# Attention stage of a four-layer graph network: which engine issues the loads of the edge weight rows

## The chip, the cores and the metric

The kernel runs on one core of a Trainium2 chip. The metric is device time in microseconds (us). The engines are TensorE (PE), VectorE (DVE), ScalarE (ACT), GpSimd (POOL) and SyncE (SP). Each runs its own instruction stream, and they meet only at semaphores. SP and ACT can issue ordinary DMAs, POOL issues the gathers whose rows are chosen by an index.

## The reference, cut to what matters

Four message-passing layers follow each other on a graph of 6250 nodes and 206250 edges, with a layer norm after each. The change lies in the fourth:

```python
w_ij = _mlp(edge_feats, rad_w0, rad_b0, rad_w1, rad_b1)
w_ij = w_ij + _mlp(chi_scalar, sph_w0, sph_b0, sph_w1, sph_b1)
q = (node_feats @ wq).reshape(-1, H, HD)[receivers]
k = (node_feats @ wk).reshape(-1, H, HD)[senders]
alpha = (q * w_ij * k).sum(axis=-1) / jnp.sqrt(jnp.float32(HD))
alpha = alpha * cutoffs[:, None]
v = (node_feats @ wv).reshape(-1, H, HD)[senders]
out = jax.ops.segment_sum(alpha[..., None] * v, receivers, num_segments=n_nodes)
```

`w_ij` does not depend on the nodes, so the kernel computes it ahead: one unit of the edge network gives the 512 rows of one group and stores them in the DRAM tensor `w_dram`.

## The kernel before

Edges are sorted by receiver and cut into 404 groups of 512 edges (4 tiles of 128). The attention stage (`attention_edges`) walks over them in 101 iterations `i` of 4 groups, `s` = 0 to 3, each with its own buffers in `kv_rows`, `w_rows`, `msgs` and `hot`. The other layers come before it; most units of the edge network are computed in them, and the last 110 in the attention stage: two in each of the first 14 iterations (`twos`), one in each of the next 82, none in the last 5. These three kinds are called the two-unit, one-unit and no-unit iterations.

What each engine does for a group `s`, in its program order:

- SP loads the weight rows of the group (256 KB, `load_w`, line 1854) once the message of the group four back is done, then the sender indices of the group four ahead (line 1849) when the gathers of this one have landed, then the receiver lanes (line 1846) when VectorE has turned the lanes before them into marks. After the four groups it stores the finished unit of the edge network (line 891) and loads the features of the next (line 882).
- POOL waits for the message of the group four back and issues four gathers of 128 key and value rows each (line 1917).
- TensorE picks the queries of the group (line 1927, waits for `hot_t` and for the message two back), adds up the messages of the group before (line 753), and does a quarter of the edge network. In a one-unit iteration that is, for `s` = 0 and 1, two of the four chunks of its first layer (line 909), and for `s` = 2 and 3 half of its second layer (line 918). In a two-unit iteration it is a whole first layer for `s` = 0 and 2 and a whole second layer for `s` = 1 and 3.
- ScalarE makes the marks of the group for the sums (`lane_hot`, lines 726 and 729, into `att_hot`), then runs Silu over the chunks that TensorE has just made (line 929, `late_hid`).
- VectorE multiplies weight rows and keys (line 2040, it waits there for the weight rows and the gathers), multiplies the queries in (line 2044, it waits for `q_done` of TensorE), reduces over heads (line 2045) and forms the message (line 2047, it counts `msg_done`). Around this it makes the windows of queries (lines 1992 and 1994), the marks `hot_t` of a group ahead (line 1984), adds finished sums into the nodes (lines 741 and 742) and finishes the edge network's rows (lines 935 and 938).

ScalarE's order in a one-unit iteration is therefore: marks 0, Silu of chunks 0 and 1, marks 1, Silu of chunks 2 and 3, marks 2, marks 3. The rows of a unit may be read only when its store has landed; SP waits for that itself, at iterations 73 and 90 and before the no-unit iterations (`mlp.stored`, `mlp.finished`).

Of the kernel before, what the change touches and what calls it, by code (L numbers as in the profile page):

```python
# [17 lines left out]
D = 128  # L18
# [3 lines left out]
T = 4  # L22
GE = T * P
S = 4
NI = -(-E // (S * GE))
# [694 lines left out]
def lane_hot(nc, act, c, s, g):  # L720

    hot = c.hot[:, s]

    act.wait_ge(c.sums_done, g + 1)
    for t in range(T):
        ins = nc.scalar.activation(hot[:, t, :], c.iota[:, 0:P], ACT.Square, scale=-1.0, bias=c.spans.lane_near[:, bass.ds(g * T + t, 1)])
    ins.then_inc(c.square_done, 1)
    act.wait_ge(c.square_done, g + 1)
    nc.scalar.activation(hot, hot, ACT.Relu, scale=-1.0, bias=1.0).then_inc(c.hot_done, 1)
# [1064 lines left out]
def attention_edges(nc, a, iota, own_lane, spans, lo_dram, w_dram, q_parts, kv_dram, acc, mlp):  # L1794


    with ExitStack() as st:
        sem = nc.alloc_semaphore

        def sb(name, shape, dt=f32):  # L1800
            return st.enter_context(nc.sbuf_tensor(f"att_{name}", shape, dt))
# [3 lines left out]
        twos, ones = 14, 96  # L1805
        units = 2 * twos + ones - twos
        assert mlp.start + units == NG

        def unit_of(i, per):
            return 2 * i if per == 2 else i + twos  # L1810
        kv_rows = sb("kv_rows", [P, S, T, 2 * D])
        w_rows = sb("w_rows", [P, S, T, D])
# [12 lines left out]
        msg_done = sem("att_msg_done")  # L1825
# [12 lines left out]
        w_in = [sem(f"att_w_in{s}") for s in range(S)]  # L1838
        lanes_in = [sem(f"att_lanes_in{s}") for s in range(S)]

        with nc.Block() as block:

            @block.sync
            def _(sp):
                def load_lanes(s, g):
                    sp.dma_start(lanes[:, s], lo_dram[bass.ds(g * GE, GE)].partition_broadcast(P)).then_inc(lanes_in[s], 16)

                def load_indices(s, g):
                    sp.dma_start(stage[:, s], a["src_tiles"][:, bass.ds(g * T, T)]).then_inc(staged[s], 16)

                def load_w(s, g):

                    sp.wait_ge(msg_done, g + 1)
                    sp.dma_start(w_rows[:, s].rearrange("p t f -> p (t f)"),
                                 w_dram[:, bass.ds(g * T * D, T * D)]).then_inc(w_in[s], 16)

                for s in range(S):
                    load_indices(s, s)
                for s in range(S):
                    load_lanes(s, s)  # L1860
                def body(i, per, first):
                    for s in range(S):
                        load_w(s, S * i + s)

                        sp.wait_ge(gathered[s], 16 * T * (i + 1))
                        load_indices(s, S * (i + 1) + s)

                        sp.wait_ge(hot_t_done, S * i + s + 1)
                        load_lanes(s, S * (i + 1) + s)
                    if per:  # L1870
                        mlp.sync_body(sp, unit_of(i, per), per, first)

                body(0, 2, True)
                with sp.Fori(1, twos) as i:
                    body(i, 2, False)
                with sp.Fori(twos, 73) as i:
                    body(i, 1, False)

                mlp.stored(sp, 80)
                with sp.Fori(73, 90) as i:  # L1880
                    body(i, 1, False)

                mlp.stored(sp, 100)
                with sp.Fori(90, ones) as i:
                    body(i, 1, False)
                mlp.store(sp, units - 1)
                mlp.finished(sp, units - 1)
                with sp.Fori(ones, NI - 1) as i:
                    body(i, 0, False)
                for s in range(S):  # L1890
                    load_w(s, S * (NI - 1) + s)

            @block.scalar
            def _(act):
                def body(i, per):
                    for s in range(S):
                        lane_hot(nc, act, c, s, S * i + s)
                        if per:
                            mlp.scalar_step(nc, act, unit_of(i, per), s, per)

                with act.Fori(0, twos) as i:
                    body(i, 2)
                with act.Fori(twos, ones) as i:
                    body(i, 1)
                with act.Fori(ones, NI) as i:
                    body(i, 0)

# [243 lines left out]
```

## Time and profile before

| | |
|---|---|
| runs | 11267.62 us, median of 3 (11256.81 to 11269.58) |
| profiled execution | 11251.21 us, its span 11249.4 us |
| granted TensorE clock | 0.828 of full speed over the span |
| busy, share of the span | PE 73%, DVE 57%, ACT 44%, POOL 28% |
| attention stage | about 8240 to 11191 us of the span |

The span is from the program's first instruction to its last. Busy time is that of an engine's own instructions; waits, branches and the issuing of DMAs by SP and ACT are not counted. A row of the timeline gives start, duration, engine, line, operation and in brackets the idle time of the engine before it with what ended it. In this kernel one and the same semaphore can serve two stages, so the name of a releaser can be that of an earlier user.

### The profile page before, as it was taken

To read this page: it belongs to the slowest core of one execution; us is meant where nothing else is said; L and a number is where in the kernel's file an instruction comes from. 1 tells how busy PE (TensorE), PEld (TensorE's weight loads), DVE (VectorE), ACT (ScalarE), POOL (GpSimd) and SP (SyncE) were. 2 spreads that over 40 slices of the span, in tenths; PEclk is the share of its full clock that TensorE was granted. 3 is DMA by queue.
4 is the path that set the end of the run, shared out by engine and by line. 5 is a ranking of instruction groups with operands and counts; after the bars stand their busy time and mean duration, and the time that the engine had idled before them with its cause. 6 is when DMAs were issued, how large, how long until landed. Compare 5 with 4: busy or idle time off the path is not lost. (4 is left out here: it accounts for less than half of the span.)

```text
span 11249.4 us, 197335 instructions
## 1 busy us (share of the span) xinstructions
PE 8246.0 (73%) x51344; PEld 6196.6 (55%) x51345; DVE 6369.1 (57%) x11872; ACT 4935.1 (44%) x9054; POOL 3183.7 (28%) x3246
## 2 busy tenths in 40 slices
PE   3888888878869999994777777777657565656654
PEld 2555555567757777773555554554435454444443
DVE  5777777789943333335555555555655555555555
ACT  2444444468745555552333333333434333333332
POOL 0000000000000000000555555555235555555554
PEclk9889888899989999996777777777778777777776
DMA  2222222256623333331111111111045445454544
GB/s 80 104 104 104 103 105 102 104 174 227 213 92 122 119 122 123 118 105 31 43 43 43 43 43 43 43 43 43 19 133 149 143 142 143 143 145 141 143 144 115
DMA packets 634626, 1180.46 MB, mean 105 GB/s; under 512 B 215640, under 2 KB 295818, under 8 KB 615011
## 3 DMA queue, kind: packets, MB, share of 16 engines
q1 hardware_dynamic: 505288, 861.87, 24.0%
q0 software_dynamic: 129280, 317.93, 10.0%
q8 instruction: 24, 0.39, 0.0%
q14 instruction: 34, 0.28, 0.0%
HBM read 902.78 MB, written 276.57 MB: 105 GB/s over the span
## 5 line engine op out<-in xcount | busy, mean ns | idle before, releaser
L1708 POOL DMA_INDIRECT conv_rows<-y_dram,conv_stage x1616 | 1550.8, 960 | 4064.3 <-issue 3399.5
L1917 POOL DMA_INDIRECT att_kv_rows<-kv_dram,att_stage x1616 | 1625.4, 1006 | 1563.0 <-DVE att_msgs L2047 845.6
L753 PE MATMUL conv_part<-conv_msgs,conv_hot 128*128 128x256 f32 x3232 | 1060.2, 486 | 159.3 <-DVE conv_msgs L1771 115.0
L929 ACT ACTIVATE late_hid<-att_mlp,late_b 128x512 f32<-128x512 f32 x440 | 282.2, 684 | 1789.3 <-remote 821.0
L1688 ACT ACTIVATE conv_hid<-conv_hid_ps 100x512 f32<-100x512 f32 x406 | 240.2, 592 | 1731.1 <-remote 866.4
L1076 DVE SCALAR_TENSOR_TENSOR mean_rest<-mean_counts,mean_high 128x896 f16<-128x896 f32 x343 | 374.7, 1093 | 1077.7 <-ACT mean_high L1037 1077.7
L1721 PEld LDWEIGHTS conv_w_ps<-conv_w,conv_hid 100*128 100x128 f32 x3240 | 509.9, 240 | 831.8 <-ACT conv_hid L1688 549.3
L918 PE MATMUL att_mlp<-late_w,late_hid 128*128 128x128 f32 x3520 | 583.0, 334 | 504.2 <-ACT late_hid L929 457.8
L753 PEld LDWEIGHTS conv_part<-conv_msgs,conv_hot 128*128 128x128 f32 x3232 | 765.3, 249 | 321.7 <-DVE conv_msgs L1771 118.1
L1721 PE MATMUL conv_w_ps<-conv_w,conv_hid 100*128 100x128 f32 x3240 | 602.4, 343 | 461.9 <-ACT conv_hid L1688 448.2
L293 PE MATMUL count_ps<-count_cols,count_rows 128*128 128x392 bf16 x3920 | 802.8, 354 | 159.2 <-DVE count_cols L259 158.3
L918 PEld LDWEIGHTS att_mlp<-late_w,late_hid 128*128 128x128 f32 x3520 | 547.8, 245 | 530.2 <-ACT late_hid L929 478.8
L2044 DVE TENSOR_TENSOR att_qk<-att_q_ps,att_qk 128x512 f32<-128x512 f32 x404 | 279.5, 692 | 950.9 <-DMA conv_scalars<-in_scalars 805.5
L753 PE MATMUL att_part<-att_msgs,att_hot 128*128 128x128 f32 x3232 | 577.9, 334 | 324.1 <-DVE att_msgs L2047 251.9
L918 PE MATMUL count_mlp<-mlp_w,mlp_hid 128*128 128x128 f32 x4704 | 691.0, 315 | 142.5 <-DVE mlp_w L938 140.5
L918 PEld LDWEIGHTS count_mlp<-mlp_w,mlp_hid 128*128 128x128 f32 x4704 | 678.9, 230 | 189.4 <-issue 166.3
L1123 PE MATMUL mean_sum_ps<-wh,mean_turned 128*128 128x129 f32 x4802 | 696.5, 285 | 51.9 <-ACT mean_turned L1045 51.3
L293 PEld LDWEIGHTS count_ps<-count_cols,count_rows 128*128 128x128 bf16 x3920 | 380.1, 103 | 642.2 <-issue 449.1
L318 ACT ACTIVATE count_counts<-count_ps 128x784 f32<-128x784 f32 x392 | 322.7, 823 | 864.6 <-PE count_ps L293 857.8
L753 PEld LDWEIGHTS att_part<-att_msgs,att_hot 128*128 128x128 f32 x3232 | 501.5, 237 | 364.0 <-issue 198.4
L259 DVE TENSOR_SCALAR count_cols<-cols,col_key 128x784 bf16<-128x784 f16 x1960 | 687.0, 419 | 0.0
L577 PE MATMUL soft_ps<-wh,soft_weights 128*128 (+1 forms) x4802 | 579.9, 280 | 142.7 <-DVE soft_weights L521 142.7
(278 smaller groups left out, 16499.4 us busy)
## 6 DMA issues: line engine op xcount, KB each, us to landing
c_dram<-count_counts SPq DMA_DIRECT2D x392, 392.0 KB, 2.4
mean_counts<-c_dram SPq DMA_DIRECT2D x343, 448.0 KB, 3.6
att_w_rows<-w_dram SPq DMA_DIRECT2D x404, 256.0 KB
soft_counts<-c_dram SPq DMA_DIRECT2D x98, 1024.0 KB, 4.8
w_dram<-mlp_w SPq DMA_DIRECT2D x294, 256.0 KB, 2.5
mlp_feats<-in_feats SPq DMA_DIRECT2D x295, 192.0 KB, 2.7
soft_counts<-c_dram SPq DMA_DIRECT2D x49, 1088.0 KB, 5.0
att_lanes<-lo_dram SPq DMA_DIRECT2D x404, 128.0 KB
```

Source lines behind the costliest of these rows:

```text
L259: ins = nc.vector.tensor_scalar(c.cols[:, b, t], at.cols[:], at.col_key[:, bass.ds(first + t, 1)], None, ALU.is_equal)
L293: ins = nc.tensor.matmul(c.ps[:, b, h, 0:CW // 2], rows, cols[:, h * (CW // 2):(h + 1) * (CW // 2)], start=first, stop=last)
L318: nc.scalar.activation(c.counts[:, v % 4].rearrange("p (h c) -> p h c", h=2), ps, ACT.Copy).then_inc(c.copied, 1)
L577: ins = nc.tensor.matmul(place(m), weights[:, b, m * P:(m + 1) * P], win(wh, w), start=False, stop=False, skip_group_check=True)
L753: ins = nc.tensor.matmul(part, c.hot[:, s, t, :], rows[:, t, :], start=half == 0 and t == 0, stop=half == 1 and t == T - 1)
L918: ins = nc.tensor.matmul(self.w_ps[:, t * D:(t + 1) * D], self.hid[:, n, t * P:(t + 1) * P], self.w1[:, n, :], start=n == 0, stop=n == 2 * ...
L929: nc.scalar.activation(self.hid[:, n], self.hid_ps[:, n % 2], ACT.Silu, bias=self.b0[:, n:n + 1]).then_inc(self.hid_done, 1)
L1076: nc.vector.scalar_tensor_tensor(rest[:, m], counts[:, m], 0.25, high[:, m], ALU.mult, ALU.subtract).then_inc(rest_done, 1)
L1123: ins = nc.tensor.matmul(sum_ps[:, 0:D + 1], turned[:, h, at:at + P], x_ext[:, k, :], start=k == 0, stop=k == NW - 1)
L1708: pool.indirect_dma_start(rows[:, s, t, :], None, y_dram, bass.IndirectOffsetOnAxis(ap=stage[:, s, t:t + 1], axis=0)).then_inc(gathered[s] ...
L1721: ins = nc.tensor.matmul(w_ps[:, n, t, :], hid[:, n, t * P:(t + 1) * P], w2[:], start=True, stop=True)
L1917: pool.indirect_dma_start(kv_rows[:, s, t, :], None, kv_dram, bass.IndirectOffsetOnAxis(ap=stage[:, s, t:t + 1], axis=0)).then_inc(gathere ...
```

## The change

`load_w` goes from SP's stream to ScalarE's. There it stands behind the marks of the same group and before the Silu of the chunks. The waits for the stores of the edge network's units go with it, and the loop of the one-unit iterations is split on ScalarE where it was split on SP. SP waits for the last loads at the end.

```diff
                 def body(i, per, first):
                     for s in range(S):
-                        load_w(s, S * i + s)
-
                         sp.wait_ge(gathered[s], 16 * T * (i + 1))
                         load_indices(s, S * (i + 1) + s)
...
-                with sp.Fori(twos, 73) as i:
-                    body(i, 1, False)
-
-                mlp.stored(sp, 80)
-                with sp.Fori(73, 90) as i:
-                    body(i, 1, False)
-
-                mlp.stored(sp, 100)
-                with sp.Fori(90, ones) as i:
+                with sp.Fori(twos, ones) as i:
                     body(i, 1, False)
...
                 for s in range(S):
-                    load_w(s, S * (NI - 1) + s)
+                    sp.wait_ge(w_in[s], 16 * NI)
 
             @block.scalar
             def _(act):
+                def load_w(s, g):
+
+                    act.wait_ge(msg_done, g + 1)
+                    act.dma_start(w_rows[:, s].rearrange("p t f -> p (t f)"),
+                                  w_dram[:, bass.ds(g * T * D, T * D)]).then_inc(w_in[s], 16)
+
                 def body(i, per):
                     for s in range(S):
                         lane_hot(nc, act, c, s, S * i + s)
+                        load_w(s, S * i + s)
                         if per:
                             mlp.scalar_step(nc, act, unit_of(i, per), s, per)
...
+                with act.Fori(twos, 73) as i:
                     body(i, 1)
+
+                mlp.stored(act, 80)
+                with act.Fori(73, 90) as i:
+                    body(i, 1)
+
+                mlp.stored(act, 100)
+                with act.Fori(90, ones) as i:
+                    body(i, 1)
+                mlp.stored(act, units - 1)
```

## Rows read from the trace of the kernel before

**Rows 1.** Windows: us; busy PE, PEld, DVE, ACT, POOL; clock; DMA; GB/s.

```profile
8240.00:8689.00 449.00, 320.11 (x2211) 239.26 (x2212) 244.00 (x445) 205.87 (x416) 230.93 (x235) 0.81 0.51 148
8689.00:11061.00 2372.00, 1431.06 (x9876) 1168.52 (x9874) 1333.12 (x2462) 804.08 (x1982) 1326.46 (x1312) 0.74 0.50 143
```

**Rows 2.** Waits of VectorE, one-unit iterations; us in total, times, longest.

```profile
DVE att_qk L2044 <- DMA conv_scalars<-in_scalars: 710.8, 154, 7.1
```

**Rows 3.** Tile att_w_rows, whole trace: idle before its reader until the load landed.

```profile
  DMA att_w_rows<-w_dram: 8.0, 13
```

**Rows 4.** Timeline of one one-unit iteration, VectorE.

```profile
10020.64 0.69 DVE L2047 TENSOR_TENSOR att_msgs<-att_kv_rows,att_alpha 128x512 f32<-128x512 f32 x1
...
10024.18 0.69 DVE L2047 TENSOR_TENSOR att_msgs<-att_kv_rows,att_alpha 128x512 f32<-128x512 f32 x1
...
10029.35 0.69 DVE L2040 TENSOR_TENSOR att_qk<-att_w_rows,att_kv_rows 128x512 f32<-128x512 f32 x1
...
10031.52 0.75 DVE L2047 TENSOR_TENSOR att_msgs<-att_kv_rows,att_alpha 128x512 f32<-128x512 f32 x1
...
10039.66 0.69 DVE L2044 TENSOR_TENSOR att_qk<-att_q_ps,att_qk 128x512 f32<-128x512 f32 x1 [6.45 <-DMA conv_scalars<-in_scalars]
...
10044.94 0.69 DVE L2040 TENSOR_TENSOR att_qk<-att_w_rows,att_kv_rows 128x512 f32<-128x512 f32 x1
...
10047.66 0.69 DVE L2044 TENSOR_TENSOR att_qk<-att_q_ps,att_qk 128x512 f32<-128x512 f32 x1 [2.04 <-DMA conv_scalars<-in_scalars]
...
10049.11 0.69 DVE L2047 TENSOR_TENSOR att_msgs<-att_kv_rows,att_alpha 128x512 f32<-128x512 f32 x1
```

**Rows 5.** Timeline of the same iteration, TensorE and ScalarE.

```profile
10023.28 2.02 PE L909 MATMUL att_mlp<-late_feats,late_w 64*128 64x512 f32 x4
...
10025.33 1.26 ACT L929 ACTIVATE late_hid<-att_mlp,late_b 128x512 f32<-128x512 f32 x2 [8.21 <-issue]
...
10026.94 1.13 PE L909 MATMUL att_mlp<-late_feats,late_w 64*128 64x512 f32 x4
...
10027.78 0.63 ACT L729 ACTIVATE att_hot<-att_hot 128x512 f32<-128x512 f32 x1
...
10029.68 0.83 PE L1927 MATMUL att_q_ps<-att_q_both,att_hot_t 128*128 128x128 bf16 x12 [1.60 <-DVE att_hot_t L1984]
...
10037.97 0.69 ACT L929 ACTIVATE late_hid<-att_mlp,late_b 128x512 f32<-128x512 f32 x1 [9.56 <-issue]
10039.43 0.69 ACT L929 ACTIVATE late_hid<-att_mlp,late_b 128x512 f32<-128x512 f32 x1 [0.78 <-remote]
...
10041.32 0.63 ACT L729 ACTIVATE att_hot<-att_hot 128x512 f32<-128x512 f32 x1
...
10043.75 1.49 PE L1927 MATMUL att_q_ps<-att_q_both,att_hot_t 128*128 128x128 bf16 x12
```

**Rows 6.** Timeline of the same iteration, POOL: first and last gather of two runs.

```profile
10022.11 0.94 POOL L1917 DMA_INDIRECT att_kv_rows<-kv_dram,att_stage  x1 [2.90 <-DVE att_msgs L2047]
...
10036.83 0.95 POOL L1917 DMA_INDIRECT att_kv_rows<-kv_dram,att_stage  x1 [0.30 <-issue]
10042.58 0.94 POOL L1917 DMA_INDIRECT att_kv_rows<-kv_dram,att_stage  x1 [4.81 <-DVE att_msgs L2047]
...
10046.74 0.94 POOL L1917 DMA_INDIRECT att_kv_rows<-kv_dram,att_stage  x1 [0.30 <-issue]
```

**Rows 7.** Timeline, two-unit iterations: a weight load, and the reader that waits for it.

```profile
8374.43 0.34 SPq L1854 DMA_DIRECT2D att_w_rows<-w_dram  x1
...
8377.53 0.69 DVE L2040 TENSOR_TENSOR att_qk<-att_w_rows,att_kv_rows 128x512 f32<-128x512 f32 x1 [0.26 <-DMA att_w_rows<-w_dram]
```

**Rows 8.** Timeline of that two-unit iteration, later: query waits and the last marks.

```profile
8383.67 0.69 DVE L2044 TENSOR_TENSOR att_qk<-att_q_ps,att_qk 128x512 f32<-128x512 f32 x1 [5.45 <-DMA conv_scalars<-in_scalars]
...
8406.68 0.69 DVE L2044 TENSOR_TENSOR att_qk<-att_q_ps,att_qk 128x512 f32<-128x512 f32 x1 [5.24 <-PE att_q_ps L1927]
8407.65 0.63 ACT L729 ACTIVATE att_hot<-att_hot 128x512 f32<-128x512 f32 x1
```

More of the change, by code:

```diff
@@ L1849, in load_indices @@
                     sp.dma_start(stage[:, s], a["src_tiles"][:, bass.ds(g * T, T)]).then_inc(staged[s], 16)
[L1851 to L1855, printed above, removed]
                 for s in range(S):
@@ L1902, in _ @@
                     body(i, 2)
-                with act.Fori(twos, ones) as i:
+                with act.Fori(twos, 73) as i:
                     body(i, 1)
+                mlp.stored(act, 80)
[5 more added lines that the diff above has]
+                mlp.stored(act, units - 1)
                 with act.Fori(ones, NI) as i:
```

## The prediction

> **What bounds the kernel now.** Only the attention stage is touched. Its windows come first: two-unit iterations take 449 us for 14 (32.1 us each), one-unit ones 2372 us for 82, or 28.9 us each [rows 1]. No engine is full there: POOL and VectorE are each busy 56% of the time, ScalarE 34%, the DMA engines 50% [rows 1]. So waits bound it. VectorE's waits come next: it stands 711 us before L2044, the multiply by the picked queries [rows 2]. The releaser's name is that of an earlier user of the semaphore; by the code it is `q_done` of TensorE. Weight rows cost nothing yet: in the whole stage their reader lost 8.0 us to them [rows 3].
>
> The timeline of one iteration shows what the 711 us are. I count from the end of the last message of the iteration before, 10020.64 + 0.69 = 10021.33, as t = 0 [rows 4]. The period is 28.5 us here: the fourth message ends at 10049.80. Two stalls stand in it: 6.45 us before L2044 of s = 2 and 2.04 us before that of s = 3 [rows 4].
>
> The first is odd. TensorE's picks for s = 2 end at t = 9.2 and its chunks 2 and 3 at 6.7, yet VectorE starts L2044 at 18.3, and ScalarE the two Silu at 16.6 and 18.1 [rows 4, 5]. Both come just after POOL's row of twelve gathers ends, at t = 16.45 [rows 6]. The second stall has the same look: the picks end at t = 23.9, POOL's next row of four ends at 26.35, and L2044 starts at 26.3 [rows 4 to 6]. In the first 3 us of a row nothing is held: chunks 0 and 1 end at t = 3.97 and the Silu starts at 4.00 [rows 5]. I read it so: what TensorE signals from some 3 us after the start of a row of gathers arrives only when the row pauses, 0.2 to 1.9 us later. The cause is not shown; the pattern is what I use.
>
> **The change, part by part.** *SP* loses four issues of about 0.34 us per iteration [rows 7] and the order they imposed. SP holds up nobody I can name, as indices and lanes are loaded a group or more ahead: nothing, and it would cost nothing back. The waits for the stores, now on ScalarE, stand before iterations 73 and 90 and before the no-unit ones, for units long stored: three waits, under 1 us each. In the five no-unit iterations the marks run ahead of VectorE: nothing.
>
> *ScalarE* gets four issues, about 0.35 us each with their register work. It is busy a third of the time; I count the 0.35 us only where a chain runs through it. Queued behind each issue are the next Silu and marks, for which TensorE waits.
>
> *The load's lead* is the real change. A load needs 3.1 us from issue to its reader's start (8374.43 to 8377.53) [rows 7]. Below, 2.8 us is left without the 0.34 us of its issue; above, one gather's cadence more, (10036.83 - 10022.11) / 11 = 1.3 us [rows 6], for a load that shares the DMA engines with a row of gathers: 4.4 us. I take 3.1, the measured one. ScalarE issues it when the last step of the marks has started. Walk through the one-unit iteration:
>
> - s = 1: the last step of the marks starts at 10027.78, t = 6.45 [rows 5]. Issue 6.8, landed 9.9. The reader wanted it at t = 8.0 [rows 4]: a new wait of 1.9 us. The message of s = 1, which ended at 10.94, ends at 12.8.
> - That opens the row of gathers. Eight of twelve are done at t = 11.2 (twelve end at 16.45, the last four take 5.1 us like the row of four [rows 6], with a 0.2 us start). POOL restarts 0.78 us after a message [rows 4, 6], at 13.6: a pause of 2.4 us. The held signals arrive in it, up to 1.65 us after its start, as before (39.43 against 37.78) [rows 5, 6]. Silu of chunks 2 and 3 starts by 12.9.
> - s = 2: from the second Silu to the last step of the marks it took 41.32 - 39.43 = 1.9 us [rows 5]. So issue at 12.9 + 1.9 + 0.35 = 15.1, landed 18.2. L2040 then and L2044 0.7 us later, at 18.9, against 18.3 before. The stall of 6.45 us is thus not won: the weight rows take its place, 0.6 us later. The message ends at 21.05 (before 20.5).
> - s = 3: L2040 follows the message by 3.15 us as before (10044.94 against 10041.8) [rows 4], at 24.2; its rows landed at about 21. TensorE has had chunks 2 and 3 activated since 13.6, so the picks for s = 3, formerly ending at 23.9, end by 20, in the pause between the row that ends at 18.8 and the message of s = 2. The 2.04 us stall is gone: L2044 at 24.9, message done at 27.05.
>
> The period falls from 28.47 to 27.05 us, by 1.4 us; times 82, -115 us.
>
> *Two-unit iterations.* The load for s = 3 is issued after marks whose last step starts at 8407.65 [rows 8], so it lands at 8411.1, and L2044, which started at 8406.68, starts at 8411.9: +5.2 us. But the next iteration's L2044 waits 5.45 us for the picks [rows 8], which TensorE then has done meanwhile. That gives about 5.4 back. The wait of 1.9 us at s = 1 I carry over whole. Net +1.7 us, times 14, +24 us; ends 0 and 14 x 7.1 = +99 us if nothing is given back.
>
> Sum: -115 + 24 = -91 us on the profiled execution's 11251.2 us (span 11249.4), 11160. The median of the runs lies 16.4 us above that execution, so **11177 us**.
>
> **A rule that speaks against it.** The weight rows would now arrive last at s = 1 and 2 of each one-unit iteration, where before the whole stage lost 8.0 us to them [rows 3]. The Trainium skill, "DMA: Bandwidth & Descriptors", Rules for kernel authors, asks to issue a DMA early and wait late, so that its fixed cost lies beside other work. By that rule the change only loses. The same table says that spreading DMAs over engines brings no bandwidth and saves issue time alone; with the DMA engines half idle I count no bandwidth either.
>
> **Rivals.**
>
> 1. *The row of gathers doesn't pause* (slower). If the load for s = 1 lands by about t = 8.5, the pause is shorter than the 1.65 us that the second Silu needed; or signals stay held through it. Then the second Silu starts at 18.1 as before, the load for s = 2 is issued at 20.35 and lands at 23.45, L2044 starts at 24.15 instead of 18.3, +5.8 us; the 2.04 us of s = 3 go: +3.8 us x 82 + 24 = +336, **11604 us**. For it: 16 gathers are POOL's constant work, and the load may be issued up to a microsecond sooner than here. Against: 1.9 us of new wait stand in the rows.
> 2. *The hold moves forward* (slower). With the period shorter, the row of s = 2 ends at 26.9 and the next starts at 27.8, a pause of 0.9 us where it was 2.9 us [rows 6]. If chunks 0 and 1 are then held too, their Silu starts at 12.9, the load of s = 1 lands at 18.2, that of s = 2 at 21.7, the last message ends at 30.6: +2.1 us x 82 + 24 = +196, **11464 us**.
> 3. *Fewer loads beside the gathers, no hold of chunks 2 and 3* (faster). The load that SP issued at the start of the row is gone. If the hold sets in after t = 6.7, the load of s = 2 lands by 13, and the stall moves to s = 3, whose picks are held until the merged row ends at about 23.9: last message at 26.1, -2.4 us x 82 + 24 = -173, **11095 us**.
> 4. *No change in kind*: the weight rows hide in the stalls and the waits trade places, 0 x 82 + 0 to 24, **11268 to 11290 us**.
>
> **Chances.** The forecast 0.35, rival 3 0.13, rival 4 0.12, rival 2 0.18, rival 1 0.22. About 0.2% (22 us) is what a measurement of this kernel can tell from no change. The faster cases are 0.48; of rival 4 and the edges of the others 0.11 is the same; slower 0.41. The forecast's own range is 11120 to 11240, the period shorter by 2.1 to 0.6 us: the landing of 2.8 to 4.4 us moves the s = 2 step by -0.3 to +1.3. The range of 8 in 10 runs from 11070 to 11580: it holds rivals 2 and 3 and half of rival 1, which lies by what share of the iterations fall into it.
>
> **What would show it.** Right: in one-unit iterations VectorE waits before L2040, not L2044, about 1.9 us at s = 1 and longer at s = 2; POOL's rows are of eight, four and four gathers; Silu of chunks 2 and 3 near t = 12; no stall at s = 3; a period near 27. In two-unit iterations a wait of some 10 us before the last L2040 and none before the first L2044. Wrong: rows of twelve still there with L2040 of s = 2 near t = 23; Silu of chunks 0 and 1 later than t = 5; or no waits for `att_w_rows` at all.

## The result: slower by 1.7%

The kernel before takes 11,265.8 us (median of 4 runs, 11,256.8 to 11,269.6), the changed one 11,455.0 us (4 runs, 11,440.7 to 11,473.8). The ratio is 1.017, 95% interval 1.0152 to 1.0188; a second measurement gave 1.0188, 1.0171 to 1.0205. The forecast was 11,177 us with a range of 11,070 to 11,580: wrong side, inside the range.

The profiled execution of the changed kernel has a span of 11,451.1 us at a granted clock of 0.820, against 11,249.4 us at 0.828. First the windows of its two-unit and one-unit iterations (us; busy time and count by engine; clock; DMA share; GB/s), which answer to [rows 1]:

```profile
8265.00:8795.00 530.00, 344.06 (x2244) 256.41 (x2244) 245.13 (x445) 210.62 (x422) 234.45 (x236) 0.77 0.43 126
8795.00:11261.00 2466.00, 1549.40 (x9839) 1266.37 (x9840) 1345.46 (x2462) 814.33 (x1963) 1321.00 (x1312) 0.74 0.48 137
```

VectorE, ScalarE and POOL do the same work in more time. Iteration by iteration, from the end of one fourth message to the next, a two-unit iteration takes 36.8 us instead of 31.2 (mean of the last 13), a one-unit one 30.07 instead of 28.92 (mean of 82): 13 x 5.6 = 73 and 82 x 1.15 = 94 us. The first two-unit iteration adds about 7 us. The remaining 27 us lie ahead of the attention stage, whose first message ends at 8248.4 us in one profile and at 8274.9 in the other. Over the twelve profiles of this condition (below), of kernels whose code is the same up to there, that moment lies anywhere from 8236 to 8283, and the earliest belongs to a kernel that contains the change. I count it as chance.

VectorE's waits in the one-unit iterations (us in total, times, longest) answer to [rows 2], and the idle time before the reader of the weight rows in the whole trace to [rows 3]:

```profile
DVE att_qk L2040 <- DMA att_w_rows<-w_dram: 412.2, 131, 8.3
DVE att_qk L2044 <- DMA conv_scalars<-in_scalars: 216.5, 67, 5.8
DVE att_qk L2044 <- DVE att_qk L2040: 75.0, 150, 0.9
```

```profile
  DMA att_w_rows<-w_dram: 623.4, 160
```

711 us before L2044 became 217, and the weight rows, which cost 8 us, cost 623. A new small term stands in the third line: where L2040 has to wait, L2044 starts 1.2 us after it and not 0.7.

One one-unit iteration of the changed kernel, all engines, answers to [rows 4 to 6]. t = 0 is 10149.40, the end of the last message before it (start us, duration, engine, line, what was waited for):

```profile
10148.71 0.69 DVE L2047 TENSOR_TENSOR att_msgs<-att_kv_rows,att_alpha 128x512 f32<-128x512 f32 x1
10156.25 0.34 ACTq L1882 DMA_DIRECT2D att_w_rows<-w_dram  x1
10159.20 0.69 DVE L2040 TENSOR_TENSOR att_qk<-att_w_rows,att_kv_rows 128x512 f32<-128x512 f32 x1 [1.69 <-DMA att_w_rows<-w_dram]
10161.93 1.26 ACT L929 ACTIVATE late_hid<-att_mlp,late_b 128x512 f32<-128x512 f32 x2 [5.19 <-remote]
10163.29 0.95 POOL L1917 DMA_INDIRECT att_kv_rows<-kv_dram,att_stage  x1 [2.57 <-DVE att_msgs L2047]
10164.53 0.34 ACTq L1882 DMA_DIRECT2D att_w_rows<-w_dram  x1
10170.61 0.69 DVE L2040 TENSOR_TENSOR att_qk<-att_w_rows,att_kv_rows 128x512 f32<-128x512 f32 x1 [7.84 <-DMA att_w_rows<-w_dram]
10171.78 0.69 DVE L2044 TENSOR_TENSOR att_qk<-att_q_ps,att_qk 128x512 f32<-128x512 f32 x1 [0.47 <-DVE att_qk L2040]
10177.06 0.69 DVE L2040 TENSOR_TENSOR att_qk<-att_w_rows,att_kv_rows 128x512 f32<-128x512 f32 x1
10177.78 0.69 DVE L2044 TENSOR_TENSOR att_qk<-att_q_ps,att_qk 128x512 f32<-128x512 f32 x1
```

The reader sees the forecast's chain nearly to the tenth: load of s = 1 at t = 6.85, its reader at 9.8 after a wait of 1.69 us, POOL pausing 2.57 us, the Silu of chunks 2 and 3 at 12.5, the load of s = 2 at 15.1, no stall at s = 3. One item differs: the load issued at 10164.53 has its reader at 10170.61, 6.1 us later. This iteration takes 30.5 us, where 27.05 was forecast. In the next one (t = 0 is 10179.92) POOL's next row starts only 0.89 us after the last, and the hold reaches s = 0 and 1:

```profile
10180.70 0.95 POOL L1917 DMA_INDIRECT att_kv_rows<-kv_dram,att_stage  x1 [0.89 <-issue]
10185.17 0.69 DVE L2044 TENSOR_TENSOR att_qk<-att_q_ps,att_qk 128x512 f32<-128x512 f32 x1 [4.35 <-DMA conv_scalars<-in_scalars]
10186.59 1.27 ACT L929 ACTIVATE late_hid<-att_mlp,late_b 128x512 f32<-128x512 f32 x2 [17.24 <-remote]
10189.18 0.34 ACTq L1882 DMA_DIRECT2D att_w_rows<-w_dram  x1
10191.95 0.69 DVE L2040 TENSOR_TENSOR att_qk<-att_w_rows,att_kv_rows 128x512 f32<-128x512 f32 x1
```

These two kinds take turns through the whole stage. I call an iteration held when its first Silu starts later than t = 5, one of the forecast's signs of being wrong. That is so in 41 of the 82 one-unit iterations, against 7 in the kernel before, and in 78 of the 81 steps from one iteration to the next the kind changes. Of the 41 held ones 38 begin with a pause of POOL of 0.9 us; of the other 41, 38 begin with one of over 2 us and none with one of 0.9. Held ones take 30.5 us on average, the others 29.7.

And a two-unit iteration (t = 0 is 8466.94, the end of the last message before it), which answers to [rows 7, 8]. At 35.7 us it is one of the four shortest:

```profile
8468.31 0.69 DVE L2044 TENSOR_TENSOR att_qk<-att_q_ps,att_qk 128x512 f32<-128x512 f32 x1 [0.50 <-DVE att_qk L2040]
8474.75 0.34 ACTq L1882 DMA_DIRECT2D att_w_rows<-w_dram  x1
8477.68 0.69 DVE L2040 TENSOR_TENSOR att_qk<-att_w_rows,att_kv_rows 128x512 f32<-128x512 f32 x1 [2.57 <-DMA att_w_rows<-w_dram]
8481.48 0.35 DVE L1984 TENSOR_SCALAR att_hot_t<-att_lanes,own_lane 128x512 bf16<-128x512 bf16 x1
8483.64 0.01 SPq L882 DMA_DIRECT2D late_feats<-in_feats  x1
8496.01 0.63 ACT L729 ACTIVATE att_hot<-att_hot 128x512 f32<-128x512 f32 x1
8496.15 0.34 ACTq L1882 DMA_DIRECT2D att_w_rows<-w_dram  x1
8499.30 0.69 DVE L2040 TENSOR_TENSOR att_qk<-att_w_rows,att_kv_rows 128x512 f32<-128x512 f32 x1 [9.72 <-DMA att_w_rows<-w_dram]
```

In the same stretch of the kernel before (t = 0 is 8376.99, the two-unit iteration of [rows 8]):

```profile
8390.39 0.69 DVE L2040 TENSOR_TENSOR att_qk<-att_w_rows,att_kv_rows 128x512 f32<-128x512 f32 x1
8393.17 0.35 DVE L1984 TENSOR_SCALAR att_hot_t<-att_lanes,own_lane 128x512 bf16<-128x512 bf16 x1
8395.31 0.01 SPq L882 DMA_DIRECT2D late_feats<-in_feats  x1
```

The load of s = 1 and the last one are waited for, 2.57 and 9.72 us; from the features' load to the last marks both kernels take the same 12.3 to 12.4 us.

### The profile page after: what moved, and what is told of

Same layout as the page of the kernel before. It is cut to its first block and busy times, and to the rows that moved or that the text cites. A ratio compares the mean times of both kernels' runs of the same rounds, so it can differ in the third digit from the quotient of the medians.

```text
span 11451.1 us, 197356 instructions
## 1 busy us (share of the span) xinstructions
PE 8425.7 (74%) x51344; PEld 6323.4 (55%) x51345; DVE 6383.9 (56%) x11872; ACT 4959.5 (43%) x9054; POOL 3179.3 (28%) x3246
## 5 line engine op out<-in xcount | busy, mean ns | idle before, releaser
L753 PE MATMUL conv_part<-conv_msgs,conv_hot 128*128 128x256 f32 x3232 | 1089.8, 497 | 221.2 <-DVE conv_msgs L1771 198.9
L753 PE MATMUL att_part<-att_msgs,att_hot 128*128 128x128 f32 x3232 | 652.6, 365 | 739.0 <-DVE att_msgs L2047 658.3
L753 PEld LDWEIGHTS att_part<-att_msgs,att_hot 128*128 128x128 f32 x3232 | 563.6, 263 | 793.5 <-DVE att_msgs L2047 611.4
L918 PE MATMUL count_mlp<-mlp_w,mlp_hid 128*128 128x128 f32 x4704 | 690.8, 315 | 142.6 <-DVE mlp_w L938 140.5
L918 PEld LDWEIGHTS count_mlp<-mlp_w,mlp_hid 128*128 128x128 f32 x4704 | 678.8, 230 | 189.5 <-issue 166.3
L918 PE MATMUL att_mlp<-late_w,late_hid 128*128 128x128 f32 x3520 | 638.4, 346 | 142.8 <-issue 136.4
L918 PEld LDWEIGHTS att_mlp<-late_w,late_hid 128*128 128x128 f32 x3520 | 601.5, 260 | 164.7 <-issue 157.4
L577 PEld LDWEIGHTS soft_ps<-wh,soft_weights 128*128 128x128 f32 x4802 | 553.0, 193 | 169.8 <-issue 167.1
```

The source lines that it names most:

```text
L577: ins = nc.tensor.matmul(place(m), weights[:, b, m * P:(m + 1) * P], win(wh, w), start=False, stop=False, skip_group_check=True)
L753: ins = nc.tensor.matmul(part, c.hot[:, s, t, :], rows[:, t, :], start=half == 0 and t == 0, stop=half == 1 and t == T - 1)
L918: ins = nc.tensor.matmul(self.w_ps[:, t * D:(t + 1) * D], self.hid[:, n, t * P:(t + 1) * P], self.w1[:, n, :], start=n == 0, stop=n == 2 * ...
```

## The experiments

My theory after the result: the loss is the lead of the load alone, in each stage. Rivals: ScalarE's queue costs something by itself; breaking POOL's rows of gathers costs; what I called held signals isn't real. One thing has to be said ahead, since the numbers can't be read without it: the measurements met the machine in two conditions. In condition A the kernel before takes 11,245 to 11,266 us, in condition B (e5 to e8 and g1 to g4) 10,013 to 10,023 us. So each time is compared only with the kernel before of its own measurement, by the ratio. Some expectations below put the conditions down to two chips. That didn't hold: e5 to e8 found 10,013 us and f1 to f4 found 11,259 us on chip 1.

**First four, in condition A.** The load ahead of the marks of its group (e1), one group ahead behind the marks of the group before (e2), on SP's queue but behind the marks (e3), and on ScalarE only outside the two-unit iterations (e4).

```
e1                                        e2, ScalarE's body
+  load_w(s, S * i + s)                      lane_hot(nc, act, c, s, S * i + s)
   lane_hot(nc, act, c, s, S * i + s)     -  load_w(s, S * i + s)
-  load_w(s, S * i + s)                   +  load_w((s + 1) % S, S * i + s + 1)
e3, SP's body, one-unit iterations, behind indices, lanes and (s = 3) mlp.sync_body
+  sp.wait_ge(c.hot_done, S * i + s + 1)
+  load_w(s, S * i + s)
e4, ScalarE                               e4, SP
+  if per < 2:                            +  if per == 2:
       load_w(s, S * i + s)               +      load_w(s, S * i + s)
```

> The load of the weight rows stays on ScalarE's queue, but is issued ahead of the marks of its group instead of behind them. In the changed kernel the one-unit iterations take 30.1 us (28.9 before), the two-unit ones 36.8 (31.2 before). Theory lead: the loss is that the rows are asked for too late. The marks are some 1.5 to 1.9 us long, so the wait before L2040 of s = 1 falls from about 1.9 to 0.4 us and that of s = 2 by 1.9 us; two-unit iterations gain 1.9 us at s = 3. Sum: 82 x 2 to 3 and 14 x 1.9 us less, 11190 to 11270 us, about as before or under it. Theory queue: what costs is that ScalarE issues the four loads at all (the issues stand in its chain, or its queue's loads land later, 5.7 us instead of 3.1 in part of the iterations). Then the place hardly matters: 11430 to 11470 us.

> ScalarE issues the load of group g + 1 behind the marks of group g: same queue, same number of issues, one group more of lead. Theory lead: nearly every wait for weight rows goes (433.8 us in 132 waits in the one-unit stretch of the changed kernel). In one-unit iterations the rows for s = 2 are then asked for at about t = 7 and those for s = 3 at about 15, so the picks decide again: 28 to 29 us an iteration; two-unit 31 us or less. Sum 11180 to 11290 us. Theory queue: 11400 us or more, with long landings still in the trace. Theory of the held signals as the main loss (the row of twelve gathers is broken, and the breaks do harm by themselves): rows of eight and four stay only if a wait at s = 1 stays, so this run can't tell it from lead unless rows of twelve are back and the time is not.

> The kernel before with one edit: in the one-unit iterations SP's queue issues the load only after the marks of the same group are done, behind the index and lane loads of its group. Two-unit iterations as before. Theory lead: as slow in these iterations as the changed kernel, about 30.1 us each, so 11266 + 82 x 1.2 = 11365 us, and the waits of L2040 on weight rows are some 400 us again. Theory queue: ScalarE issues nothing here, so the time stays at 11266 us, within 20.

> The change for the one-unit and no-unit iterations only; in the two-unit iterations SP loads the weight rows as before. If the two losses add up, two-unit iterations are back at 31.2 us and one-unit ones stay at 30.1: 14 x 5.6 = 79 us less than the changed kernel, about 11375 us. If what the two-unit iterations lose is given back by the first one-unit ones or comes from elsewhere, the time stays above 11420. In the profile of the changed kernel the attention stage also starts 26 us later than in that of the kernel before, though nothing ahead of it is changed: if that is chance, the starts of these four runs scatter between 8236 and 8263 us whatever the kernel; if it belongs to programs whose ScalarE code is longer, the three kernels with loads on ScalarE start late and the one with SP's queue early.

| kernel | us | ratio to before, interval | two-unit | one-unit | held, of 82 |
|---|---|---|---|---|---|
| before (iterations from the first profile) | 11,261 | 1 | 31.2 | 28.92 | 7 |
| changed, second time (f1) | 11,470 | 1.0188 (1.0171 to 1.0205) | 36.8 | 30.10 | 42 |
| e1 ahead of the marks | 11,357 | 1.0083 (1.0066 to 1.0099) | 33.4 | 29.54 | 30 |
| e2 one group ahead | 11,265 | 1.0001 (0.9991 to 1.0010) | 31.7 | 28.75 | 11 |
| e3 SP, behind marks | 11,349 | 1.0086 (1.0065 to 1.0107) | 31.5 | 29.86 | 45 |
| e4 not in two-unit | 11,385 | 1.0101 (1.0084 to 1.0118) | 31.4 | 30.40 | 43 |

e2 and e3 decide between queue and lead. With four issues per iteration still on ScalarE, but one group earlier, the whole loss is gone. With nothing on ScalarE's queue, but the load behind the marks, a one-unit loss is there: 29.86 us. It is a near copy and not an exact one, as SP also comes late to s = 0: 42 of its 184 waits for weight rows stand there, where the changed kernel has none. Their weight-row waits, e2 (whole trace) and e3 (one-unit iterations):

```profile
  DMA att_w_rows<-w_dram: 35.3, 19
```

```profile
DVE att_qk L2046 <- DMA att_w_rows<-w_dram: 419.7, 184, 6.1
```

e4 took back the two-unit part, 0.7 to 0.9% (78 to 98 us), and no more. In e3 the 45 held iterations take 30.9 us and the other 37 take 28.6, no more than the same kind in the kernel before (28.7). So late loads cost time also by holding the first Silu of every second iteration. e1 missed its lead number (11,190 to 11,270): the marks' 1.9 us more of lead bring half of the loss back, so each us of lead is not worth a us of time. e2 also shows that full lead wins nothing over the kernel before: the stall before L2044 is back (563.8 us in its one-unit iterations) as soon as the weight rows are not later than the picks.

**Which load.** With e2 as base, one load is put back behind its own marks: s = 3 of the two-unit iterations, s = 2 or s = 1 of the one-unit ones. The first two ran in both conditions, the third in B.

```
+  if per == 2 and s == 3:                      # s = 2 and s = 1: per == 1
+      load_w(s, S * i + s)
+  if (s < S - 1 or not last) and not (per == 2 and s == 2):
       load_w((s + 1) % S, S * i + s + 1)
```

> Base is the run with the loads one group ahead on ScalarE (11265 us, two-unit iterations 31.7 us). Only in the two-unit iterations, and there only for s = 3, the load stands behind the marks of its own group again, as in the changed kernel. If that one load carries the two-unit loss: 36 to 37 us an iteration, 14 x 5 = 70 us more, 11335. If the next iteration gives the time back, as the prediction had it, or the loss needs all four loads: 11265 to 11290 us.

> Same base; only in the one-unit iterations, and there only for s = 2, the load stands behind the marks of its own group (base: 28.75 us an iteration). If the load of s = 2, whose marks stand behind the late Silu of chunks 2 and 3, carries the loss: 30 us or more, 11365 us or more; with the row of twelve left whole and the Silu held to its end it could reach 32 us, 11500. If the loss comes from s = 1: 11265 to 11290 us.

> Loads one group ahead on ScalarE, but in two-unit iterations that of s = 3 behind its own marks, once more. On a chip that holds signals: if this load carries the two-unit loss, 70 us over the run with all loads ahead, ratio 1.006; if the time is given back, 1.000 to 1.002. On a chip that doesn't: 1.0036 again.

> Loads one group ahead on ScalarE, but in one-unit iterations that of s = 2 behind its own marks, once more. On a chip that holds signals: the wait at s = 1 that broke the row of twelve is gone, so the Silu of chunks 2 and 3 stays held to the row's end and the load of s = 2 behind it: 31 to 32.5 us an iteration, ratio 1.018 to 1.03, more than the whole change costs. If the row breaks all the same: 1.005 to 1.012. On a chip that doesn't hold: 1.0185 again.

> Loads one group ahead on ScalarE, but in one-unit iterations that of s = 1 behind its own marks (with s = 2 so: 29.74 us an iteration against 28.75 without, ratio 1.009; the whole change: 30.1). If the two add up: 0.4 to 0.6 us an iteration, ratio 1.003 to 1.006. If s = 1 costs its own 1.9 us in full, 1.014. If the stall behind it hides it, 1.000 to 1.002. Where no signals are held: 1.000 to 1.004.

| load late | ratio, A | iteration, A | ratio, B |
|---|---|---|---|
| s = 3, two-unit | 1.0047 (1.0030 to 1.0064) | 35.9 (base 31.7) | 1.0036 (1.0022 to 1.0051) |
| s = 2, one-unit | 1.0091 (1.0072 to 1.0109) | 29.74 (base 28.75) | 1.0185 (1.0168 to 1.0202) |
| s = 1, one-unit | not run | | 1.0014 (1.0005 to 1.0024) |

In two-unit iterations the one load of s = 3 makes 4.1 of the 5.1 us that lie between e2 and the change. In one-unit iterations that of s = 2 makes 1.0 of 1.35. The load of s = 1, where the forecast had put a new wait of 1.9 us, is worth some 14 us in all in B (5 to 24). The kernel with all loads ahead wasn't measured by itself in B, so the ratios there are to the kernel before. f4 came out under its forecast of 1.018 to 1.03: 25 of its one-unit iterations take 31.8 us, as expected for a row left whole, but the other 57 are held ones of 28.9 us. So the 1.0 us of s = 2 is reached there by another mix of iterations than in the changed kernel.

**Are signals held?** Here POOL gets a wait on TensorE's picks, so that its row of gathers breaks for a reason that has nothing to do with weight rows: before one group in four (e5, f2) or before every group (e6, g1, h1). The loads stay on SP's queue.

```
       pool.wait_ge(msg_done, S * i + s + 1)
+      if not first:                       # e5, f2: and s == 1
+          pool.wait_ge(q_done, S * i + s - 1)
```

> The kernel before (weight rows on SP's queue) with one wait more: POOL starts the second group's gathers of an iteration only when TensorE has signalled its picks for s = 2 of the iteration before, so the row of twelve gathers breaks into eight and four for a reason that has nothing to do with weight rows. Theory held signals: what TensorE signals during a long row of gathers arrives only when the row pauses. The pause at t = 11.2 lets the picks and both chunks through, the stall of 6.45 us before L2044 of s = 2 shrinks to 1 us or less: 3 to 5 us less for each of 82 iterations, 10850 to 11020 us. Rival: the picks really are late, or POOL has no slack and each pause is paid for: 11266 us or up to 1 us an iteration more, 11350.

> As the run with one such wait, but before each group's gathers POOL waits for the picks of three groups earlier, so no row is longer than four gathers unless the signal has come. Held signals: as much as with one wait or up to 1 us an iteration more, from the 2.04 us stall at s = 3; 10800 to 11020 us. Rival: pauses are paid for, 11300 us or more.

> The kernel before with POOL waiting for TensorE's picks before one of four groups of gathers, once more. On a chip that holds the signals: 3 to 5 us less an iteration, ratio 0.963 to 0.98. On one that doesn't: 0.998, as in the first run. Rival, that POOL's pause gains nothing even where signals are held: 1.00 or more.

> The kernel before with POOL waiting, before each group's gathers, for TensorE's picks of three groups earlier; once more, its first run fell into the state where no signal is held (ratio 1.000 there). Where signals are held: with one such wait the stall before L2044 went from 6.45 to about 1 us at s = 2 and came back at s = 3 (L2040 at t = 18.8, L2044 at 25.3), 1.0 us an iteration was won. Theory held signals: with every row broken the one at s = 3 goes too, 3 to 5 us an iteration, 10850 to 11010 us, ratio 0.964 to 0.978. Rival, that the stall is only handed on, or POOL's pauses are paid for: 0.99 to 1.005. Where no signals are held: 1.000 again.

> The kernel before with POOL waiting before each group's gathers for TensorE's picks of three groups earlier, for the state where signals are held. With one such wait 1.0 us an iteration was won and the stall came back at s = 3. Theory held signals: with every row broken it goes there too, ratio 0.964 to 0.985. Rival, handed on once more or paid for in POOL's pauses: 0.99 to 1.005. Where no signals are held: 1.000, as twice before.

Condition A: one wait 0.9961 (0.9947 to 0.9975), all waits **0.9718 (0.9701 to 0.9734), 10,927 us**, one-unit iterations of 25.4 us. Condition B: 0.998 (0.9970 to 0.9989) with one wait, 1.000 twice with all. With one wait the stall leaves s = 2 and comes back at s = 3, 6.0 us long (f2, VectorE; in order s = 2, then s = 3):

```profile
9863.58 0.69 DVE L2050 TENSOR_TENSOR att_qk<-att_q_ps,att_qk 128x512 f32<-128x512 f32 x1 [1.30 <-DMA conv_scalars<-in_scalars]
...
9875.76 0.69 DVE L2050 TENSOR_TENSOR att_qk<-att_q_ps,att_qk 128x512 f32<-128x512 f32 x1 [6.00 <-DMA conv_scalars<-in_scalars]
```

So my expectation of 3 to 5 us from one wait was wrong; with all waits it holds, 3.5 us. The hold isn't gone then: the same kernel's one-unit iterations take 25.4 us in A and 21.2 in B, and in A 210 of its 328 batches of chunks are still signalled more than 0.5 us after their end. VectorE's wait before the multiply by the picks in the one-unit iterations of f2, and then of h1 (L2050 is the L2044 of the kernel before):

```profile
DVE att_qk L2050 <- DMA conv_scalars<-in_scalars: 544.3, 132, 6.0
```

```profile
DVE att_qk L2050 <- DMA conv_scalars<-in_scalars: 153.4, 107, 4.2
```

Condition B shows gathers without the hold. g1 there, one-unit iterations: the chunks of TensorE, the Silu behind them and POOL's gathers, one every 1.3 us without a break:

```profile
8856.91 0.95 POOL L1919 DMA_INDIRECT att_kv_rows<-kv_dram,att_stage  x1 [0.30 <-DVE att_msgs L2053]
8857.69 1.13 PE L909 MATMUL att_mlp<-late_feats,late_w 64*128 64x512 f32 x4
8858.17 0.95 POOL L1919 DMA_INDIRECT att_kv_rows<-kv_dram,att_stage  x1 [0.30 <-issue]
8858.85 1.26 ACT L929 ACTIVATE late_hid<-att_mlp,late_b 128x512 f32<-128x512 f32 x2
8859.42 0.95 POOL L1919 DMA_INDIRECT att_kv_rows<-kv_dram,att_stage  x1 [0.30 <-issue]
```

The Silu starts 1.2 us after the start of its chunks, in the middle of the gathers; in the kernel before in condition A it started 11.0 us after it [rows 5]. The groups of TensorE's second layer in the one-unit iterations (busy us, mean ns, idle us before), first of the kernel before in condition A, then of g1 in B:

```profile
L918 PE MATMUL att_mlp<-late_w,late_hid 128*128 128x128 f32 x2648 | 475.8, 351 | 488.3 <-ACT late_hid L929 457.8 <-issue 30.0
```

```profile
L918 PE MATMUL att_mlp<-late_w,late_hid 128*128 128x128 f32 x2652 | 423.8, 329 | 0.0
```

These are two kernels; f3 and e7 are one and the same in A and B. The idle time before L918 is 348.1 us in f3 and 0.0 in e7, and VectorE's wait for the picks (L2049 there) is this in f3 and doesn't occur in e7:

```profile
DVE att_qk L2049 <- DMA conv_scalars<-in_scalars: 550.2, 129, 6.6
```

From the end of a batch of chunks to TensorE's semaphore event pass 6.7 us in f3 (median of 328 batches in the one-unit iterations) and 0.01 us in e7, at most. The granted clock differs too, 0.74 and 0.85 there. But TensorE's busy time differs by 209 us and the stretches by 632, so a slower TensorE could make up a third of it at most.

**Lead or broken rows.** Last, the changed kernel again, the changed kernel with all of POOL's waits (g2, h2), and e2 with them (g4).

> The changed kernel itself, once more. In the runs so far the kernel before took 11261 us on one chip and 10013 us on another: on the first, TensorE's signals that fall into a row of gathers come 2.5 to 5 us late (median), on the second 0.01 us, and POOL's gathers run there without a break, a one-unit iteration in 20 to 22 us. On a chip of the first kind: ratio 1.017 as before. On one of the second kind there is no late Silu, and the load of s = 2 alone, late, cost 2.2 us an iteration there (ratio 1.0185); with s = 1 and the two-unit iterations beside it theory lead expects 1.02 to 1.035, 10210 to 10360 us. Rival, that the change loses only through the held signals: 1.00 to 1.01 there.

> The changed kernel with the same waits of POOL. Theory lead: weight rows are still late at s = 1 and s = 2 and in two-unit iterations, so it stays 100 to 250 us above the run g1 whatever the rows do. Rival, that the changed kernel loses in the one-unit iterations by its rows of gathers: it comes within 80 us of g1 (the two-unit part alone). Where no signals are held: theory lead 1.02 to 1.035 against the kernel before.

> Loads one group ahead on ScalarE and POOL's waits of g1 together. Weight rows are never late, so only held signals and POOL's pauses are left: as g1 or up to 50 us less. A load issued in a pause of POOL and landing in 2.6 to 3.1 us changes nothing, since nobody waits for it. If g4 is above g1 by more than 30 us, ScalarE's issues themselves cost something after all.

> The changed kernel with the same waits of POOL. Theory lead: 100 to 250 us above h1 where signals are held (238 us above the kernel before where they are not). Rival, that the broken rows are what costs: within 80 us of h1.

Condition A: h2 takes 11,121 us, 0.9897 (0.9881 to 0.9914), 194 us above h1 of the same measurement. Condition B: g2 takes 10,261 us, 1.0241 (1.0224 to 1.0258), 243 us above g1. So the change costs about as much where rows are already broken and where nothing is held: lead, not rows. (The changed kernel without POOL's waits wasn't measured in B.) Between h1 and h2 the two-unit iterations go from 29.2 to 37.4 us and the one-unit ones from 25.4 to 26.5, 14 x 8.2 + 82 x 1.1 = 205 us. g4 is 1.0004 (0.9995 to 1.0014) where g1 is 0.9999 (0.9989 to 1.0008): 10 us apart with overlapping intervals, so four issues on ScalarE cost nothing that can be told from none. VectorE's waits in the one-unit iterations of h2:

```profile
DVE att_qk L2046 <- DMA att_w_rows<-w_dram: 288.5, 117, 8.7
```

The version that beats both kernels is h1, SP's queue and POOL's waits: 318 us faster than the kernel before in condition A, the same in B.

## Why the prediction was wrong, step by step

- **What bounds it, and the held signals.** Right, as far as tested. The pattern read from one iteration was good enough to predict where rows would break and when the Silu would start, and a kernel built on it alone won 2.8%. The edge of "some 3 us" isn't clean, in the rows themselves: the chunks that pass at once end 3.2 us into their row (25.30 against 22.11), the picks for s = 3, which are held, end 2.7 us into theirs (45.24 against 42.58) [rows 5, 6]. That the pattern belongs to one condition of the machine, the single profile could not show.
- **ScalarE's issues at nothing, SP's at nothing.** Right: e2 1.0001, g4 10 us from g1.
- **s = 1 of one-unit iterations.** Right in place and size in the iteration shown: a wait of 1.69 us (1.9 forecast), a pause of POOL of 2.57 (2.4), Silu at 12.5 (by 12.9). Over the stage 52 of 82 iterations wait there. The stall at s = 3 is gone in this iteration and on average only halved, 1.2 us instead of 2.6.
- **The landing of the load of s = 2: the first step that failed in the one-unit sum.** I took 3.1 us, with 4.4 as upper end. In the iteration shown it measured 6.1 us from issue to reader, in a load issued 1.2 us after a row of four gathers had begun. The forecast's own pause causes this: the load follows the Silu, the Silu follows the pause, so it is issued just as gathers begin. The 3.1 us of [rows 7] came from a load that SP issued elsewhere in its schedule. In the changed kernel as well, 3.15 us is the time of a load after the gathers have ended (8496.15 to 8499.30). 3.0 us of landing and 0.5 us from L2040 to L2044 (1.17 us, not 0.7) are the whole difference between 27.05 and 30.5 us here. Over the 41 iterations that aren't held the landing is 5.1 us on average, and they take 29.7 us. The gathers alone don't make it so long: in e3's one-unit iterations 53 awaited loads that SP issued 0.8 to 3 us into a row took 2.95 us (median). ScalarE's loads follow each other more closely; 36 of the changed kernel, issued at this place with the next one within 2.5 us, took 5.4 us, and 38 with such a follower, but outside a row, 2.9. Nor does the loss need the long landing: in e3 no awaited load of s = 2 took over 3.8 us, and its iterations take 29.86 us.
- **The hold moving forward (rival 2, chance 0.18).** This is the second step that failed. It came in 41 of the 82 iterations, the second shown among them: POOL's pause of 0.89 us (0.9 forecast), L2044 of s = 0 held 4.35 us, Silu at t = 6.7 (12.9 forecast). The forecast treated it and the main case as alternatives, but they take turns, and the short pause of POOL between an iteration's last row and the next one's first goes with the held kind. The held iterations miss the forecast's 27.05 by more than the others, 30.5 us against 29.7, with a landing of 3.0 us at s = 2. Rival 2's 11,464 us is near the measured 11,455 by luck, as its composition is another: it had +2.1 us in one-unit iterations and +1.7 in two-unit ones, and the trace has +1.15 and +5.6. The range holds the result only because it was stretched over rival 2 and half of rival 1. Rival 1 never came: no one-unit iteration has its second pair of Silu later than t = 14.1 (18.1 in rival 1).
- **Two-unit iterations: the give-back failed.** The +5.2 us at s = 3 came. And the wait of 5.45 us at the next s = 0 did go (L2044 at t = 1.4). But the time didn't reach the end of the iteration. L2040 of s = 1 starts at t = 10.7 (13.4 before), since its row is issued at 7.8 behind four Silu and the marks; `att_hot_t` of s = 3 at 14.5 (16.2 before); SP issues the features of the second unit at 16.7 (18.3 before), and from there to the last marks the time is the same. So 1.6 us of 5.4 are handed on, and the last load hangs behind those marks: issue, landing and message put 6.6 us behind them (1.2 before). Marks, load, message, features and Silu form a closed loop that the load was not in before. That makes +3.8 us in this iteration. Of the 13 iterations, the four whose second pair of Silu starts by t = 5.4 take 35.1 to 35.7 us, the nine where it starts at 5.7 to 7.4 take 36.7 to 38.2. f3 shows it with one load moved: 35.9 us instead of 31.7. I had summed the waits of VectorE without following the features' load through SP and the Silu to the next marks.
- **The rule against the change.** [rows 3] with 8 us became 623 us. The Trainium skill, "DMA: Bandwidth & Descriptors", Rules for kernel authors, asks to issue a DMA early and wait for it late. By that rule the change loses, and the runs agree: the changed kernel, e1 and e2 differ in nothing but how early they issue, and lose 1.7 to 1.9, 0.8 and 0.0%. Slower had deserved more than the 0.41 I gave it.

Of the 189 us, two-unit iterations hold some 80 (profiles; up to 98 by e4) and one-unit ones about 94.

## What to carry to other kernels

Before a load is moved, look at how much slack its reader has now, and at what runs when the load will be issued: here two of the loads, each put behind the last thing that TensorE and ScalarE finish in a round, cost 0.47% and 0.91% one at a time, where the whole change costs 1.7 to 1.9%. When a wait is removed, follow its time along the chain to the next round's same instruction before it is called given back; a load put at the end of that chain closes a loop. A stall that one engine's row of DMAs sets on others can be tested by making that engine wait once per group: one added wait mostly moved the stall, four won 2.8% in condition A and nothing in B.

## What the runs showed of the hardware

- The same kernel took 11,245 to 11,266 us in some measurements and 10,013 to 10,023 us in others. In the first condition most of what TensorE signals from 2 to 3 us on into a row of POOL's indirect gathers reaches ScalarE and VectorE only about when the row pauses (6.7 us late, median of the chunks in f3); in the second it passes at once (0.01 us in e7, the same kernel). The conv stage, which gathers in the same way, ends there some 500 us earlier too (first message of the attention stage at 7714 to 7731 us instead of 8236 to 8283). Whether the signals are held or the engines' instructions come late stays open. For the second speaks that TensorE too loses its pace in a long row: two single matmuls of a batch 0.71 us apart in f2, where [rows 5] has the batch of 12 in one.

```profile
9873.48 0.22 PE L1933 MATMUL att_q_ps<-att_q_both,att_hot_t 128*128 128x128 bf16 x1 [0.46 <-issue]
9874.19 0.22 PE L1933 MATMUL att_q_ps<-att_q_both,att_hot_t 128*128 128x128 bf16 x1 [0.50 <-issue]
9875.59 1.23 PE L1933 MATMUL att_q_ps<-att_q_both,att_hot_t 128*128 128x128 bf16 x10 [1.18 <-issue]
```

- What sets the condition wasn't found; no edit of mine did, since the kernel before has both times, and the chip alone doesn't either, since chip 1 showed both. The granted clock over the span is 0.82 to 0.84 in the first and 0.88 in the second; whether as cause or as consequence isn't shown.
- In the first condition a load of weight rows (256 KB) takes about 3 us from issue to reader outside a row of gathers, and about as long inside one when no other weight load follows it closely (2.95 us, median of 53 in e3). Issued 0.8 to 3 us into a row, with the next load within 2.5 us behind it, it took 5.4 us (median of 36 in the changed kernel). This is no fixed rule: with POOL's waits (h2) 37 such loads took 3.5 us. That loads and gathers share the DMA engines is a possible reason, and not shown.
